# A causal attention block with FFN: VectorE adds up the second short chunk's probabilities too, and one step of features moves from slot 6 to slot 8

## The reference

```
paths = sigmoid(x @ Wp + bp)                      # 5 numbers per head and token
agree = pq * pk + (1 - pq) * (1 - pk)
sim   = cumprod(agree, axis=-1).sum(axis=-1) / 5  # masked to -inf above the diagonal
attn  = softmax(sim)                              # exp(sim) / sum of exp(sim)
x = layernorm(x + (attn @ (x @ Wv)) @ Wo)
h = silu(x @ wg.T) * (x @ wu.T)
x = layernorm(x + h @ wd.T)
```

## Time and profile before

| | before |
|---|---|
| median of 3 runs | 843.91 us (843.62 to 843.93) |
| profiled execution, its own time | 842.06 us |
| its span, first to last instruction | 840.2 us |
| granted TensorE clock, mean | 0.996 of full speed |
| PE busy | 799.7 us, 95% |
| DVE busy | 607.2 us, 72% |
| ACT busy | 456.6 us, 54% |
| POOL busy | 290.0 us, 35% |

### The profile page before, as it was taken

One profiled execution on the slowest core, in us unless ns is written; L12 is line 12 of the kernel. 1 busy time (PEld: TensorE's weight loads), 2 busy tenths in 40 slices (PEclk: granted clock), 3 DMA queues, 4 the chain that ended last, 5 costly groups with the idle time before them and its releaser, 6 DMA issues.

```text
span 840.2 us, 14486 instructions
## 1 busy us (share of the span) xinstructions
PE 799.7 (95%) x5570; PEld 396.8 (47%) x5570; DVE 607.2 (72%) x1097; ACT 456.6 (54%) x721; POOL 290.0 (35%) x266
## 2 busy tenths in 40 slices
PE   6999999999999999999999999999999999899986
PEld 5553364454644446443554536445364444444253
DVE  2767966779667776679765796667966777757677
ACT  1656736557365554656546564565736556455522
POOL 0101522336225262243522453133622426224324
PEclk9999999999999999999999999999999999999999
DMA  7832462033710625006540056202370042600001
GB/s 224 200 117 76 101 156 97 1 92 85 176 51 1 147 76 151 30 2 151 118 133 1 26 126 151 101 1 75 88 190 1 1 116 75 163 1 2 26 1 52
DMA packets 47510, 71.02 MB, mean 85 GB/s; under 512 B 3920, under 2 KB 26704, under 8 KB 47440
## 3 DMA queue, kind: packets, MB, share of 16 engines
q1 hardware_dynamic: 47440, 70.07, 32.0%
HBM read 53.28 MB, written 16.78 MB: 83 GB/s over the span
## 4 chain that ended last, share of the span: by engine, by line
PE 58%; DVE 25%; issue 9%; ACT 5%; DMA 1%; POOL 1%; SPq 0%; DVEq 0%; POOLq 0%; ACTq 0%
PE slot L885 10%; PE misc L967 9%; PE ctx_ps L908 9%; PE misc L859 7%; PE misc L954 7%; PE misc L931 6%; DVE acc L606 6%; PE den_ps L914 5%; DVE work L706 5%; ACT probs L510 3%; DVE x L689 3%; DVE acc L603 2%; DVE x1T_lo L696 2%; PE misc L868 2%; DVE ctx_raw L616 1%
## 5 line engine op out<-in xcount | busy, mean ns | idle before, releaser
L510 ACT ACTIVATE probs<-slot 128x1024 f32<-128x1024 f32 (+3 forms) x384 | 290.2, 808 | 290.6 <-PE slot L885 264.5
L439 POOL TENSOR_SCALAR_AFFINE_SELECT probs<-probs 128x512 f32<-128x512 f32 x128 | 142.3, 1112 | 210.0 <-ACT probs L510 209.9
L453 POOL TENSOR_TENSOR work<-work 128x512 f16<-128x512 f32 x96 | 116.2, 1211 | 163.7 <-ACT work L528 163.7
L908 PE MATMUL ctx_ps<-probs,vz_sb 128*32 128x512 f32 (+3 forms) x1536 | 163.9, 499 | 2.6 <-DVE ctx_raw L616 2.6
L885 PE MATMUL slot<-query_stack,key_stack 128*128 128x512 f16 (+3 forms) x768 | 161.3, 332 | 1.6 <-ACT probs L510 0.8
L954 PE MATMUL misc<-x1T_hi,w_parts 128*128 128x512 f16 x358 | 135.9, 379 | 8.0 <-DVE x1T_lo L696 5.9
L954 PE MATMUL misc<-x1T_lo,w_parts 128*128 128x512 f16 x358 | 135.7, 379 | 0.0
L885 PEld LDWEIGHTS slot<-query_stack,key_stack 128*128 128x128 f16 x768 | 56.9, 98 | 160.9 <-issue 128.3
L706 DVE SCALAR_TENSOR_TENSOR work<-work,misc 128x512 f32<-128x512 f32 x90 | 61.4, 682 | 59.8 <-ACT work L522 59.8
L606 DVE TENSOR_TENSOR acc<-acc,probs 128x1536 f32<-128x1536 f32 (+3 forms) x60 | 98.9, 1649 | 0.0
L444 POOL TENSOR_TENSOR rstd<-var_eps,neg_half 128x4 f32<-128x4 f32 x31 | 31.4, 1013 | 158.9 <-DVE var_eps L661 135.4
(11 more groups left out here) (81 smaller groups left out, 735.2 us busy)
## 6 DMA issues: line engine op xcount, KB each, us to landing
key_stack<-phi_dram SPq DMA_DIRECT2D x56, 256.0 KB, 5.7
query_stack<-phi_dram SPq DMA_DIRECT2D x56, 256.0 KB, 6.7
x_sb<-in_x_dram SPq DMA_DIRECT2D x8, 1024.0 KB, 5.5
out_dram<-x SPq DMA_DIRECT2D x15, 512.0 KB, 4.0
xT_sb<-in_xT_dram SPq DMA_DIRECT2D x7, 1024.0 KB, 5.0
phi_dram<-phi_hi SPq DMA_DIRECT2D x14, 256.0 KB, 2.0
phi_dram<-phi_lo SPq DMA_DIRECT2D x14, 256.0 KB, 2.3
key_stack<-phi_dram SPq DMA_DIRECT2D x16, 128.0 KB, 3.1
```

Source lines behind the costliest of these rows:

```text
L439: pool.affine_select(out=tile, in_=tile, compare_op=ALU.is_ge, fill=0.0, base=0, pattern=[[0, 4], [1, P]], channel_multiplier=-1).then_inc ...
L453: pool.tensor_tensor(hid_lo[:, n % M1, :], hid[:, n % HSLOTS, :], hid_hi[:, n % M1, :], ALU.subtract).then_inc(hid_lo_ready, 1)
L510: act.activation(probs[:, s % P_SLOTS, 2 * p:2 * p + 2, off:CH], slot[p][:, :, off:CH], ACT.Exp).then_inc(slot_drained[p], 1)
L908: mm = pe.matmul(ctx_ps[32 * k:32 * k + 32, off:CH], vz_sb[:, b % 2, j, 32 * h:32 * h + 32], probs[:, s % P_SLOTS, k, off:CH], start=first ...
```

## The change

Chunk 1 joins the chunks that VectorE adds up, from its first key block on, in every batch but batch 0. The first addition (step 5) copies the 128 columns of step 4 that step 5 lacks, and adds the other 384; steps 6 and 7 are added in place with 256 and 128 columns. For this chunk the sums stand behind the table's work of their slot, in slots 6, 7 and 8. TensorE leaves out the 4 matmuls with `ones` in each of the steps 4 to 7 and does 4 matmuls of `acc` in slot 9, which start the accumulation (`start=alone`). The second half's features move from slot 6 to the end of slot 8, ahead of that slot's sum. The counting of the semaphores follows.

```diff
-    ADD_FROM = {2: 3, 3: 1}
+    ADD_FROM = {1: 0, 2: 3, 3: 1}
...
-    SUM_END = {(b, q): max(i for i in ADDED if STEPS[i][0] == q and not (b == B - 1 and q == NQ - 1 and i in DIAG))
-               for b in range(B) for q in ADD_FROM}
+
 
     def added(b, i):
-        return i in ADDED and i <= SUM_END[b, STEPS[i][0]]
-    NA = len(ADD_FROM)
+        q, c, g, j = STEPS[i]
+        return i in ADDED and not (b == 0 and c == 0) and not (b == B - 1 and q == NQ - 1 and i in DIAG)
+
+    SUM_END = {(b, q): max(i for i in ADDED if STEPS[i][0] == q and added(b, i))
+               for b in range(B) for q in ADD_FROM if any(STEPS[i][0] == q and added(b, i) for i in ADDED)}
+    SUMS = {at: n for n, at in enumerate((b, i) for b in range(B) for i in ADDS if added(b, i))}
+    SUMMED = {at: n for n, at in enumerate(SUM_END)}
...
-        6: turn_x1(-1, 1) + [("load_xT", 2), ("bias", 1, 1), ("squash", 1, 1), ("features", 1, 1)],
+        6: turn_x1(-1, 1) + [("load_xT", 2), ("bias", 1, 1), ("squash", 1, 1)],
         7: gate_pair(-1, 6),
-        8: gate_pair(-1, 7) + halves(-1, 6),
+        8: gate_pair(-1, 7) + halves(-1, 6) + [("features", 1, 1)],
...
-        if s >= 1 and (s - 1) % NS in ADDS and added(*divmod(s - 1, NS)):
-            plan += [("sum", *divmod(s - 1, NS))]
-        plan += between(b, i)
+        sums = [("sum", *divmod(s - 1, NS))] if s >= 1 and divmod(s - 1, NS) in SUMS else []
+        short = (s - 1) % NS < TC * NG
+        plan += between(b, i) + sums if short else sums + between(b, i)
...
                         i2 += i2 not in ADDS
-                        act.wait_ge(summed, len(ADDS) * b2 + ADDS.index(i2) + 1)
+                        act.wait_ge(summed, SUMS[b2, i2] + 1)
...
-                    dve.tensor_tensor(acc[:, :, :], probs[:, (s - 1) % P_SLOTS, :, :], own, ALU.add).then_inc(summed, 1)
+                    if SUMMED[b, q]:
+                        dve.wait_ge(acc_used, SUMMED[b, q])
+                    first = probs[:, (s - 1) % P_SLOTS, :, :]
+                    if off:
+                        dve.tensor_copy(acc[:, :, 0:off], first[:, :, 0:off])
+                    dve.tensor_tensor(acc[:, :, off:CH], first[:, :, off:CH], own, ALU.add).then_inc(summed, 1)
...
-                if q in ADD_FROM:
-                    dve.wait_ge(acc_used, NA * b + list(ADD_FROM).index(q) + 1)
+                if (b, q) in SUMMED:
+                    dve.wait_ge(acc_used, SUMMED[b, q] + 1)
...
-                    pe.wait_ge(summed, len(ADDS) * b + ADDS.index(i) + 1)
+                    pe.wait_ge(summed, SUMS[b, i] + 1)
+                    alone = ADD_FROM[q] == 0
+                    if alone and NQ * b + q >= 1:
+                        pe.wait_ge(den_out, NQ * b + q)
                     for k in range(4):
-                        mm = pe.matmul(den_ps[32 * k:32 * k + 32, :], ones[:, :], acc[:, k, :], start=False, stop=final)
+                        mm = pe.matmul(den_ps[32 * k:32 * k + 32, :], ones[:, :], acc[:, k, :], start=alone, stop=final)
```

More of the change, by code:

```diff
@@ L592, in add_up @@
                 own = probs[:, s % P_SLOTS, :, off:CH]
-                count = len(ADDS) * b + ADDS.index(i)
+                count = SUMS[b, i]
                 if i in DIAG:
@@ L599, in add_up @@
                 if j == ADD_FROM[q] + 1:
-                    used = NA * b + list(ADD_FROM).index(q)
-                    if used:
-                        dve.wait_ge(acc_used, used)
-                    dve.tensor_tensor(acc[:, :, :], probs[:, (s - 1) % P_SLOTS, :, :], own, ALU.add).then_inc(summed, 1)
+                    if SUMMED[b, q]:
[4 more added lines that the diff above has]
+                    dve.tensor_tensor(acc[:, :, off:CH], first[:, :, off:CH], own, ALU.add).then_inc(summed, 1)
                 else:
```

## The result

The changed kernel takes 848.04 us (median of 7 runs, 846.98 to 848.44) against 843.78 us before (7 runs): ratio 1.0051, 95% interval 1.0037 to 1.0064. It is slower by about 4.3 us, where +5.6 was forecast. The profiled execution took 848.44 us with a span of 846.7.

The account below looks back on a forecast made before the run. TensorE was taken to bound slots 7 to 10, after VectorE in slot 6. Two new waits cost 0.94 us in each of six batches, batch 7 0.0, batch 0 unchanged: +5.6 us, median 849.5, range 846.0 to 853.5.

Parts of the forecast that it names:

- What bounds each slot: Slot 6 waits for VectorE's L696, then TensorE bounds through slot 10; fewer columns save 0.44 us a batch without waits.
- The durations: VectorE's new work in slots 7 and 8: copy 0.42 us, additions 1.75, 1.21 and 0.68, features 2.07.
- The first wait: Slot 7: exps(7) waits for VectorE's first addition, 240.35 instead of 238.56; slot 8's gate starts 0.14 us later.
- The second wait: Slot 9: TensorE's acc matmuls wait 0.39 us for the last addition and cost 1.06; slot 10's scores come 0.94 us later.
- Passing on: Slots 10 and 11: the 0.94 us delay passes whole, as VectorE idles 1.72 us before L636; batch 7 loses 0.0.
- The sum: Whole kernel: six batches (1 to 6) at 0.94 us each, +5.6 us in all.
- "faster" rival: Slots 7 to 9: additions hide wholly, hinging on exps(7); -0.44 us in each of 7 batches, -3.1 us, 840.8; 5%.
- The rule I had weighed for the last addition: Slot 8: GpSimd's hid_lo, issuing first, blocks the last addition; 2.9 us a batch, 861 in all; collision rival 4%.

Follow-up runs that it names:

- e4: Kernel before with chunk 1's probability sums left out in batches 1 to 7, four constant-tensor matmuls in slot 9 instead: 99.77 us a batch, 839.87 us, ratio 0.9972.
- e5: Changed kernel with the tanh ahead of exps(7) in ScalarE's order in slot 7: 101.05 us a batch, 848.09 us, ratio 1.0052 to before.
- e1: Changed kernel with the last addition ahead of the features in slot 8: 100.42 us a batch, 844.54 us, ratio 1.0022 to before.
- e9: e6 with gate 8's halves (hid_hi, hid_lo) moved from slot 10 to slot 11: 99.82 us a batch, 841.04 us, ratio 0.9959 to before.
- e6: Changed kernel with tanh ahead of exps(7) and last addition ahead of the features: 100.65 us a batch, 845.01 us, ratio 1.0021 to before.
- e8: e1 with room for 4 steps in probs instead of 3, unused weight branch cut: 100.60 us a batch, 844.36 us, ratio 1.0012 to before.
- e12: e11 with gate 8's halves back in slot 10: 100.39 us a batch, 845.01 us, ratio 1.0009 to before.
- e7: Kernel before with room for 4 steps in probs instead of 3, unused weight branch cut: 100.19 us a batch, 842.63 us, ratio 0.9993.
- e10: Kernel before with only gate 8's halves moved from slot 10 to slot 11: 100.19 us a batch, 844.11 us, ratio 0.9994.
- e11: e1 with step 4's sum left on TensorE and gate 8's halves in slot 11: 99.73 us a batch, 840.57 us, ratio 0.9956 to before.
- e3: Changed kernel with the features left in slot 6, ahead of the first addition: 103.61 us a batch, 864.76 us, ratio 1.0277 to before.

## Why the prediction was right, point by point

- **What bounds each slot.** L696 in slot 6, TensorE from slot 7 to 10: shown by e4 (0.41 us a batch for 0.44 forecast, nothing for slot 6's 512 columns).
- **The durations.** Copy 0.42 us (0.42 forecast, from a cast), first addition 1.75 (1.75), second 1.22 (1.21), last 0.68; features 2.03 to the next instruction (2.07).
- **The first wait.** exps(7) 3.60 us behind L702's start; forecast 3.58. The tanh followed it by 0.55 and not 0.65 us, so the rest of the chain was 0.1 us earlier than forecast: last addition 10.72 us behind instead of 10.82.
- **The second wait.** 0.41 us idle for 0.39 forecast, acc matmuls 1.07 for 1.06. In all 0.87 a batch for 0.94.
- **Passing on.** The delay of slot 10 appears whole in the distance from batch to batch. Batch 7, without features, takes 33.72 us from slot 6 to slot 14 (736.75 to 770.47) against 33.71 before, 0.0 as forecast.
- **The sum.** 6 x 0.87 = 5.2 us; the medians say 4.3 (3.1 to 5.4 by the interval), forecast 5.6.

Two things that I had written were incomplete, though they did not change the result. First, my reckoning gave the first wait 0.65 + 0.14 us. Alone it is worth nothing (e5), since TensorE then waits for the last addition that much longer; the second alone is worth 0.63 (101.05 to 100.42), and with the second gone and no meeting with GpSimd on either side, the first is worth 0.60 (e1 to e9). Second, my "faster" rival rested on exps(7) alone. e6 met its condition (the gate of slot 8 started 4.92 us behind x1T_lo, before 5.50, both from TensorE's timeline), and so did e8; both were slower than before: a third wait, in slot 11, lay behind the other two. The rule I had weighed for the last addition (Trainium skill, "SBUF — State Buffer", section "Who interferes with whom": the one that issues first keeps the ports for the whole instruction) struck another VectorE instruction, `normalise`'s product, and only in kernels in which TensorE was ahead (e6, e8, e12). The traces agree with it in both orders: 0.69 and 1.65 us when VectorE starts first, 1.59 and 1.16 when GpSimd does. The block is a little short of whole: if the second waited for the first's very end, e6's product would take 1.05 + 0.69 = 1.74 us and before's L453 0.62 + 1.16 = 1.78.

The profiled execution of the changed kernel was 6.4 us longer than that of before, not 5.2. Of this, 1.4 us came in the ending: the lag behind before is 4.57 us at the L712 that starts at 801.34 (796.77 before) and 5.94 at that of 823.70 (817.76). In between, TensorE's granted clock was 0.75 of full speed (817 to 822 us), at a wait of 2.81 us; before, at the same wait of 2.80 us, it stayed full. Such a fall in the ending stands in 9 of the 14 profiled executions, in those of e7 and e10 too, which have no additions for chunk 1; so this 1.4 us is not shown to be a cost of the change. On the other side, the changed kernel reached slot 6 of batch 1 0.66 us sooner. There it was the kernel before whose clock fell, to a mean of 0.72 from 74 to 80 us, at a wait of 1.72 us; the changed kernel kept full clock (1.00) at one of 1.71. The distances from batch 1 to batch 6 hold neither of the two.

## What to carry to other kernels

Before moving work to an idle engine, write down what its new instructions hold up: here not the adding but a buffer place (exps(7)) and the queue ahead of the last addition cost more than TensorE's columns brought. Idle time of an engine is only worth what its neighbours in the queue leave of it; put the instruction that another engine waits for ahead of the one that nobody waits for, and leave on the bounding engine what is hidden there anyway (e11). Waits in a row don't add up: removing the first alone gave nothing, removing the second alone gave 0.63 us a batch, and removing both uncovered a third and came out slower than removing the second alone, so take them all away before judging a change.

## What the runs showed of the hardware

- Which of two instructions starts first, by about 0.1 us, decides whether VectorE or GpSimd pays: 0.90 us more for VectorE's product in e6, none before, where GpSimd pays 0.49 off the critical path. In each of these meetings (before, e6, e12) the second instruction takes 0.13 to 0.15 us less than if it had waited for the first's end. Making TensorE faster moved the two against each other.
- TensorE's clock falls to its lower level (1.2 GHz) in some places at or behind a wait of 1.7 to 2.8 us, and not in others of the same kernel. In e6, batch 7, the gate pair behind a wait of 1.8 us took 3.52 us in place of 1.89; the granted clock between 735 and 739 us was 0.60 of full speed, so at the lower level for most of it. In batches 1 to 6 the same pair, behind a wait of 1.7 us, kept its 1.89.

```profile
734.74 3.52 PE misc L970 x8
```

- In e3 this came in three of five distances (103.7 to 104.5 us in place of 102.82). What decides when it falls stays open. The changed kernel idles longer in slot 6 (1.70 us in place of 0.84), and whether this brings more falls was not tried; its profiled execution has none there.
